# Routing from raw transposes, choices in pieces of 4 and 12 tiles, and two dense steps moved from the prefix to just ahead of the routed experts

## The reference

```
logits = xn @ Wg.T
top_v, top_i = top_k(logits, 2);  gates = softmax(top_v)
pos = running count of earlier choices of the same expert   # kept if pos < cap = 640
h = gelu(inp) * gate                # inp, gate = halves of  x_e @ W1[e]
out[token] += gate * (h @ W2[e])    # for both choices of the token
x + xn + attention(xn) + experts(xn)
```

## Time and profile before

| | |
|---|---|
| median of 3 runs | 143.52 us (142.47 to 145.86) |
| profiled execution, first to last instruction | 141.6 us |
| TensorE busy | 108.6 us, 77% |
| VectorE busy | 93.5 us, 66% |
| ScalarE busy | 68.8 us, 49% |
| GpSimd busy | 75.1 us, 53% |

### The profile page before, as it was taken

How to read it: one execution, slowest core, us unless ns; L and a number is a source line. 1 busy time by engine, 2 the same in 40 slices (tenths; PEclk the granted TensorE clock), 3 DMA queues, 4 the chain that set the end, 5 groups by cost and what they waited for, 6 DMA issues and landing times.

```text
span 141.6 us, 2294 instructions
## 1 busy us (share of the span) xinstructions
PE 108.6 (77%) x705; PEld 97.6 (69%) x705; DVE 93.5 (66%) x299; ACT 68.8 (49%) x164; POOL 75.1 (53%) x92
## 2 busy tenths in 40 slices
PE   0039999999888884898399999999999988965000
PEld 0029769788777763786298999999999987655000
DVE  0699787696576867897337587897757330463991
ACT  0478773346558751323536666767766644410000
POOL 7700707777787787770000277877877777730000
PEclk9999999999999999999959999999999999999755
DMA  3999999999511111114990011111111111696487
GB/s 98 247 329 287 284 370 326 354 347 300 163 42 59 39 64 54 44 59 108 316 283 8 0 56 37 56 58 39 56 58 58 39 56 56 191 306 187 145 237 219
DMA packets 31980, 21.35 MB, mean 151 GB/s; under 512 B 2224, under 2 KB 29872, under 8 KB 31968
## 3 DMA queue, kind: packets, MB, share of 16 engines
q1 hardware_dynamic: 29104, 16.41, 41.3%
q0 software_dynamic: 2144, 4.53, 9.5%
q10 hardware_dynamic: 720, 0.27, 0.8%
HBM read 10.04 MB, written 11.15 MB: 150 GB/s over the span
## 4 chain that ended last, share of the span: by engine, by line
PE 35%; POOL 22%; DVE 13%; issue 11%; DMA 11%; ACT 2%; SPq 1%; POOLq 1%; DVEq 0%; ACTq 0%
POOL y_rows L447 20%; PE bank_h L935 5%; DMA y_last<-rows,target_i 5%; PE bank_h L937 4%; PE bank_h L936 4%; DMA qT<-y_last 3%; PE bank_x L1105 3%; PE bank_y L1047 3%; DMA xs<-in_x 3%; PE bank_x L1016 3%; PE bank_y L956 2%; PE bank_a L956 2%; POOL y_last L447 2%; DVE pre L763 2%; DVE stats L632 2%
## 5 line engine op out<-in xcount | busy, mean ns | idle before, releaser
L447 POOL DMA_INDIRECT y_rows<-rows,target_i x30 | 30.0, 1000 | 25.6 <-ACT rows L588 17.1
L434 POOL DMA_INDIRECT x_slots<-xa,slot_i x32 | 32.6, 1019 | 14.3 <-issue 9.4
L901 DVE TENSOR_TENSOR hid<-gelu,bank_h 128x384 f32<-128x384 f32 (+2 forms) x32 | 16.3, 510 | 19.2 <-ACT gelu L605 19.1
L1157 PE MATMUL bank_y<-w_sb,hid 128*128 128x128 f32 x172 | 21.9, 276 | 2.3 <-issue 2.3
L1157 PEld LDWEIGHTS bank_y<-w_sb,hid 128*128 128x128 f32 x172 | 21.0, 191 | 2.8 <-issue 2.7
L935 PE MATMUL bank_h<-xg_hi,w_lo 128*128 128x384 f32 (+1 forms) x56 | 20.1, 359 | 1.4 <-DVE xg_lo L852 1.2
L605 ACT ACTIVATE gelu<-bank_h 128x384 f32<-128x384 f32 (+2 forms) x32 | 14.7, 459 | 12.0 <-PE bank_h L937 11.2
L937 PE MATMUL bank_h<-xg_hi,w_hi 128*128 128x384 f32 (+1 forms) x56 | 18.0, 321 | 0.0
L936 PE MATMUL bank_h<-xg_lo,w_hi 128*128 128x384 f32 (+1 forms) x56 | 17.9, 320 | 0.0
L588 ACT ACTIVATE rows<-bank_y,gate_slot 128x128 f32<-128x128 f32 x35 | 10.6, 366 | 10.7 <-PE bank_y L1157 10.7
L935 PEld LDWEIGHTS bank_h<-xg_hi,w_lo 128*128 128x128 f32 x56 | 11.1, 197 | 2.0 <-DVE xg_lo L852 1.6
(11 more groups left out here) (156 smaller groups left out, 241.0 us busy)
## 6 DMA issues: line engine op xcount, KB each, us to landing
x_slots<-vacant SPq DMA_DIRECT2D x7, 340.0 KB, 6.7
rows<-x_slots SPq DMA_DIRECT2D x7, 340.0 KB, 5.7
w_raw<-in_w SPq DMA_DIRECT2D x4, 512.0 KB, 7.3
y_rows<-zeros SPq DMA_DIRECT2D x2, 1024.0 KB, 12.2
expo<-y_rows SPq DMA_DIRECT2D x8, 256.0 KB, 7.3
xs<-in_x SPq DMA_DIRECT2D x4, 256.0 KB, 4.5
y_last<-zeros SPq DMA_DIRECT2D x1, 1024.0 KB, 10.9
qT<-y_last SPq DMA_DIRECT2D x4, 256.0 KB, 3.8
```

The source lines that it names most:

```text
L434: nc.gpsimd.indirect_dma_start(x_slots, bass.IndirectOffsetOnAxis(ap=slot_i[:, k, t:t + 1], axis=0), xa[:, t, :], None,).then_inc(rows_out ...
L447: nc.gpsimd.indirect_dma_start(y_rows if r < R - 1 else y_last, bass.IndirectOffsetOnAxis(ap=target_i[:, n:n + 1], axis=0), rows[:, n, 0:D ...
L901: nc.vector.tensor_tensor(hid[s % 2][:, c, 0:cols], gelu[i % 2][:, 0:cols], bank_h[2 * c + 1][:, 0:cols], ALU.mult).then_inc(hid_ready, 1)
L1157: ins = nc.tensor.matmul(bank_y[:, j * D:(j + 1) * D], hid[s % 2][:, c, j * P:(j + 1) * P], w2_sb[:, e, c, :], start=(c == 0), stop=(c == ...
```

## The change

- x itself is transposed as soon as it arrives (`turn_group`). The gate weights are multiplied by a centering matrix (`center`, identity minus 1/128), so that the logits of these transposes are those of xn up to a positive factor per token; the gap between the two best is scaled by `inv1` afterwards. xn is transposed as well, a second time per group, for the QKV products and the dense steps.
- Choices are made in pieces of 4 and 12 tiles. xn of tiles 0 to 7 is made on GpSimd, of 8 to 11 on VectorE, of 12 to 15 on ScalarE.
- `early_product`, `early_results` and `y_early` are gone. The steps are now: two dense, 14 routed, two dense. At the two joints TensorE finishes the step before (`down`) ahead of the next step's `transpose_slots` and `up`.
- SyncE stores the vacant slots ahead of the first weights; the first routed expert's slots are loaded in two transfers. w1's split of expert 0 moves into the QKV loop.

```
-EARLY = 2
-HALVES = 2
+LEAD = 2
+PIECES = ((0, 4), (4, 12))
-    steps = [(e, j0, nj, r) for r, (e, j0, nj) in enumerate(routed_steps)] + all_token_steps[EARLY:]
+    steps = all_token_steps[:LEAD] + [(e, j0, nj, r) for r, (e, j0, nj) in enumerate(routed_steps)] \
+        + all_token_steps[LEAD:]
+    joints = (LEAD, LEAD + len(routed_steps))
...
 TensorE, prefix
             pe.wait_ge(ident_ready, 1)
+            turn_group(0)
+            pe.wait_ge(center_ready, 1)
+            pe.wait_ge(wg_in, 16)
+            nc.tensor.matmul(bank_h[0][:, 0:E], center[:, :], wg_sb[:, :], start=True, stop=True).then_inc(wgc_raw, 1)
+            turn_group(1)
+            pe.wait_ge(wgc_ready, 1)
+            for t in range(GROUP):
+                logits_tile(t)
+            turn_group(2)
+            turn_group(3)
+            for t in range(GROUP, GROUP + 2):
+                logits_tile(t)
+            pe.wait_ge(const_ready, 1)
+            earlier_choices(0)
             transpose_group(0)
+            for t in range(GROUP + 2, T):
+                logits_tile(t)
             transpose_group(1)
+            pe.wait_ge(beta_ready, 1)
+            nc.tensor.matmul(bank_h[3][:, 0:QKV], beta_cols, wqkv_sb[:, :],
+                             start=True, stop=True).then_inc(bias_raw, 1)
             transpose_group(2)
...
             for t in range(T):
-                if t == RESULTS_AT:
+                if t == GROUP - 1:
+                    earlier_choices(1)
+                    transpose_group(3)
                     pe.wait_ge(bias_ready, 1)
-                    early_results(1)
                 qkv_tile(t)
...
 VectorE, prefix
+            statistics(0)
+            statistics(1)
+            statistics(2)
+            inverses(0)
+            statistics(3)
             dve.wait_ge(const_ready, 1)
+            dve.wait_ge(inv1_ready, 1)
             dve.wait_ge(logits_ready, 1)
             choose(0)
+            inverses(1)
+            slots(0)
             gates(0)
+            dve.wait_ge(inv1_ready, 2)
+            nc.vector.scalar_tensor_tensor(nmi[:, 3 * GROUP:T], mv[:, 3 * GROUP:T, 0], -1.0, inv1[:, 3 * GROUP:T],
+                                           ALU.mult, ALU.mult).then_inc(nmi_ready, 1)
+            normalise(2)
+            lower_transposed(0)
+            prepare_wqkv()
             dve.wait_ge(logits_ready, 2)
             choose(1)
+            lower_transposed(1)
+            slots(1)
+            gates(1)
+            dve.wait_ge(std2_ready, 1)
+            link(nc.vector.reciprocal(inv2[:, :], std2[:, :]))
+            nc.vector.tensor_tensor(inv2[:, :], inv2[:, :], std1[:, :], ALU.mult).then_inc(inv2_ready, 1)
+            lower_transposed(2)
             lower_transposed(3)
...
 GpSimd
+            for t in range(2 * GROUP):
+                nc.gpsimd.tensor_scalar(xn[:, t, :], xs[:, t, :], mv[:, t, 0:1], inv1[:, t:t + 1],
+                                        ALU.subtract, ALU.mult).then_inc(xn_pool_ready, 1)
...
 TensorE, steps
             for s in range(S):
-                if s == first_dense:
+                if s in joints:
                     down(s - 1)
+                    if steps[s][3] is not None:
+                        transpose_slots(s)
                 up(s)
-                if s >= 1 and s != first_dense:
+                if s >= 1 and s not in joints:
                     down(s - 1)
```

More of the change, by code:

```diff
@@ L86, in moe_attention_block @@
     for s in range(S):
+        if s in joints and steps[s - 1][3] is None:
+            for j in range(GROUP):
+                note_sum(("step", s - 1), (steps[s - 1][1] + j,))
         for c in range(FC):
[L88 to L95, removed]
+            if (s, c) in FIRST_IN_STEP:
+                g = FIRST_IN_STEP[s, c]
+                note_sum(("first", g), tuple(range(g * GROUP, (g + 1) * GROUP)))
+        if s >= 1 and s not in joints and steps[s - 1][3] is None:
             for j in range(GROUP):
@@ L328, in load_w1 @@
                              w1[2 * i:2 * i + 2].rearrange("e p n -> p e n")).then_inc(w1_in[i], 16)
+            sp.wait_ge(vacant_ready, 2)
+            for r in range(R):
+                sp.dma_start(x_slots_tiles[:, r, :, :], vacant[:, r % 2, :, :]).then_inc(vacant_stored, 16)
             load_w1(0)
@@ L349, in _ @@
             sp.wait_ge(rows_out, 16 * TOP_K * T)
-            for r in range(R):
+            first = PARTS[0][1]
+            sp.dma_start(rows[:, 0:first, :], x_slots_tiles[:, 0, 0:first, :]).then_inc(rows_in[0], 16)
+            sp.dma_start(rows[:, first:ST, :], x_slots_tiles[:, 0, first:ST, :]).then_inc(rows_in_late, 16)
+            for r in range(1, R):
                 sp.dma_start(rows[:, r * ST:(r + 1) * ST, :], x_slots_tiles[:, r, :, :]).then_inc(rows_in[r], 16)
@@ L513, in _ @@
[L513 to L519, removed]
+            nc.scalar.activation(std2[:, :], mv[:, :, 1], ACT.Sqrt, scale=1.0 + LN_EPS,
+                                 bias=eps_sq[:, 0:1]).then_inc(std2_ready, 1)
+            turned(2)
@@ L520, in _ @@
+            nc.scalar.activation(unused[:, :], eps[:, :], ACT.Exp)
+            gap_power(0)
+            turned(3)
+            upper_transposed(0)
+            normalise(3)
             upper_transposed(1)
-            early_gelus(0, 0)
+            act.wait_ge(bias_raw, 1)
+            nc.scalar.activation(bias[:, 0:2 * D], bank_h[3][:, 0:2 * D], ACT.Copy, bias=1.0)
+            nc.scalar.activation(bias[:, 2 * D:QKV], bank_h[3][:, 2 * D:QKV], ACT.Copy).then_inc(bias_ready, 1)
+            gap_power(1)
@@ L968, in earlier_choices @@
+            def earlier_choices(i):
+                pe.wait_ge(assigned_ready, i + 1)
+                before = before_bank[i]
+                t0, nt = PIECES[i]
+                nc.tensor.matmul(before, earlier[:, :], assigned[:, t0:t0 + nt, :], start=True, stop=False)
+                for t in range(t0 + nt - 1):
                     first = max(t + 1, t0)
                     ins = nc.tensor.matmul(before[:, first - t0:, :], ones_bf[:, :],
-                                           assigned[:, t:t + 1, :].broadcast_to((P, t0 + TH - first, E)),
```

413 lines of the change are left out of this document (161 added, 252 removed).

## The result

The changed kernel takes **147.14 us** (median of 4 runs, 146.25 to 148.37), the kernel before, run beside it, 143.00 (4 runs, 141.81 to 145.86). The ratio is 1.028 with a 95% interval from 1.020 to 1.036: slower by 4.1 us, with the lower end of the interval just under two per cent (1.0198). The profiled executions span 145.9 us against 141.6, so +4.3, and the rest of this document accounts for that. In every series the kernel before is run again beside the others, its runs fall into a faster and a slower group, and a ratio is formed from the faster runs alone.

What follows compares the result with a forecast made beforehand. The prediction took GpSimd's result scatters to bound the kernel: first scatter, plus 44.25 us, plus 17.0 of tail. Dense steps +10.6, prefix −3.8 and clock −1.0 gave +5.8, so 143.5 became 149.3 us, range 146.0 to 153.0.

Steps and rivals of the forecast that it cites:

- The dense steps ahead: Between attention and routed steps: two dense steps of 11.2 us, less 0.6 of covered wait, delay the slots' transposes by 10.6.
- The prefix: Before the QKV loop and at its start: the attention ends 3.8 us earlier, bounds 0.6 and 6.6; first product 2.6 earlier.
- The clock ahead of the routed steps: After the attention: dense work without waits may remove the granted clock's dip, gaining 0 to 1.9 us, taken as 1.0.
- Sum to the first scatter: Start of the first result scatter: +10.6 − 3.8 − 1.0 = +5.8 us, with scatters and tail shifting along.
- The earlier slots: Slot scatters before the routed steps: they end near 60 to 62, but 10 us of cover makes this count nothing.
- The predicted gap between the pieces' scatters: On GpSimd, between pieces 0 and 1: a new wait for slots(1), gates(1) and ScalarE's xn at some 29 us.
- What bounds the kernel: At the end: start of first result scatter, plus 44.25 us of scatters, plus 17.0 of tail; TensorE cannot shorten them.
- VectorE and GpSimd side by side: In the prefix, `choose(0)` beside GpSimd's normalisations: one VectorE stall of 0.7 us, from none to three (0 to 2.1) possible.
- A: Rival: the slots set the routed start, transposes come at 65, and the change is faster at 139.3 us; chance 4%.
- B: Rival: VectorE never waits in the prefix and the clock dip is gone, 145.6 us, within 2%; chance 14%.
- C: Rival: the prefix gains nothing, eaten by logits, transposes and stalls; +10, 153.5 us; chance 12%.

Runs made afterwards that it cites:

- e4: The changed kernel with 20 and 8 idle products, results never read, put into TensorE's two waits in the prefix: 145.02 us, ratio 1.013 to the kernel before.
- e1: The changed kernel with all four dense steps behind the routed ones: 146.64 us, ratio 1.029 to the kernel before.
- e8: The changed kernel without its two dense steps ahead of the routed ones (expert 0 for tokens 0 to 1023 not computed): 138.42 us, one run.
- e7: The kernel before without its last two dense steps (expert 0 for tokens 1024 to 2047 not computed): 143.61 us, one run.
- e2: The changed kernel without its two last dense steps (expert 0 for tokens 1024 to 2047 not computed): 143.32 us, one run.
- e6: The changed kernel with all dense steps last, VectorE's adds of fetched rows moved earlier, and 28 idle products in the prefix: 140.92 us, ratio 0.985 to the kernel before.
- e3: The kernel before with only its dense steps moved as in the change, logits, choices and slots as before: 148.11 us, ratio 1.037 to the kernel before.
- e9: The changed kernel, dense order unchanged, with VectorE's adds of fetched rows moved into and ahead of the last dense steps: 145.86 us, one run.

## Why the prediction was right, and where it was not

The forecast was 149.3 us, from 146.0 to 153.0, with 0.82 on slower. The time is 147.14, and it is slower. Taken by its own steps:

- **The dense steps ahead**, +10.6: measured +10.3 (10.89 from the attention's end to the transposes, less the 0.59 that stood there before). The four pieces at the end of the trace were a fair model of the same pieces in the middle, wait for VectorE's adds included. (The prediction put the transposes at 69.16 + 5.8; it should have been 69.16 + 6.8, since the clock's term lies behind them; the sum is not touched.)
- **The prefix**, −3.8: measured −4.64. This is the term that was mis-sized, and inside it two errors nearly cancelled. The first product came 5.5 us earlier, not 2.6, since TensorE's queue for the second piece took 10.5 us and not 12.2 and began 0.9 earlier: VectorE had no stall in `choose(0)`, and transposes, logits, bias and QKV tiles were each a little cheaper. Of that, 0.8 was given back: from the first product to the attention's end the kernel took 35.7 us, before 34.8. e4 says to what, since with the clock kept up it was 32.9. I had costed the clock only for the QKV tiles ahead of the counting, not for the idle stretch behind them.
- **The clock ahead of the routed steps**, −1.0: measured −1.03 from transposes to first scatter (10.12 instead of 11.15). The granted clock behind the transposes' start was 0.66 before (70 to 74) and 1.00 after (74 to 82); in e1 and e8, with no dense step in between, it fell there again (0.57, 0.63 from 66 to 70).
- **Sum to the first scatter**, +5.8: measured +4.63, and the span +4.3.
- **The earlier slots**, nothing: measured nothing. The predicted gap between the pieces' scatters did not appear; slot loads started at 60.67.
- **What bounds the kernel**: here the prediction was only half right. It took the scatters for the one chain that sets the end, and wrote that TensorE "may run ahead of the scatters". TensorE does not run ahead at the end: its last product and VectorE's tail are a second chain, level with the first within 1.2 us before (e7) and 2.3 above it after (e2). The forecast came out because the two lead steps delay both alike, and that was luck: the same reasoning would have promised 135 us for e1, and 144.2 came.
- **VectorE and GpSimd side by side.** The prediction added one stall of 0.7 for VectorE. `choose(0)`'s operations ran at 0.15 to 0.27 beside GpSimd's normalisations, so there was none. The Trainium skill, "SBUF — State Buffer", section "Who interferes with whom", has a VectorE instruction with two SBUF inputs contend with a GpSimd instruction that reads SBUF. In this trace VectorE hardly paid: one operation of `slots(0)` took 0.39 where its neighbours took 0.18 and 0.19. GpSimd took 0.78 us for a normalisation that VectorE does in 0.34; what GpSimd takes for it undisturbed no run here shows.

The trace of the kernel before showed the second chain already, in VectorE's timeline:

```profile
129.55 1.12 DVE L884 SCALAR_TENSOR_TENSOR xs<-bank_y,gate_dense,xs 128x128 f32<-128x128 f32 x4 [2.16 <-PE bank_y L1157]
...
136.87 1.53 DVE L788 TENSOR_TENSOR xs<-xs,qT 128x512 f32<-128x512 f32 x2 [0.18 <-DMA qT<-y_last]
```

VectorE waits for TensorE's last product, adds without a wait, and then stands only 0.18 us for the rows of the last scatters. That short wait is all by which the scatters were the later of the two.

The rivals: A's mechanism is real but far off. The slots would set the start at 63.3 (e6), only once the attention ends before that with nothing ahead. The prediction's argument that the attention cannot end under 62 was a little too strong: it ended at 60.84 in e6. B would have needed TensorE's clock to stay up in the prefix: e4, at 1.013 (1.002 to 1.024), lies within two per cent by its middle. C, a prefix that gains nothing, is refuted by the trace, where the attention ends 4.64 earlier.

Why the change loses is then plain: in the prefix two dense steps cost 5.2 us at the attention's end (e3), so by the difference about half of their 11 us must have lain in time that TensorE would have stood idle. Ahead of the routed experts they cost 9.2 (e8), all of it in both chains. The difference of 4.0 is close to the 4.3 between the spans.

## What to carry to other kernels

When the end is read from one chain, shorten that chain on paper and see which row waits next: here a second chain lay within 1 to 2 us of it, and a rule that fitted both traces failed at the first edit that moved the two apart. Work that fills an engine's idle time is cheap where it stands; before moving it out, price it by what it delays there (5.2 us), not by its own length (11). And look at the clock behind every idle stretch that a change leaves on TensorE: filling two of them with 28 idle products made the kernel 2.1 us shorter by the medians.

## What the runs showed of the hardware that was not expected

Products whose result is never read paid for themselves here: 20 of 512 columns and 8 more kept the granted clock at 1.00 where it was 0.50 to 0.68, and the kernel was 2.1 us shorter by the medians and 2.6 by the spans. The Trainium skill, "TensorE: Matmul & The Clock Gate", section "What's actually happening", says that activity releases the throttle. The trace agrees: 0.91 us of work in the 4 us from 24 to 28 is followed by 0.68 and 0.50, and in e4 4.00 us of work in the same stretch is followed by 1.00.

The clock is also a matter of luck at the margin: at the attention's start (50 to 54) it was 0.58 in the changed kernel, 0.57 in e8 and 1.00 in e1, e2 and e9, with the same program up to there. From VectorE's first product to the attention's end that made 35.7 us against 34.3 to 34.7. In e7, which has the prefix of the kernel before, the clock fell to 0.59 from 58 to 62, where it had been 1.00, and the attention ended at 71.20 instead of 68.57; 2.1 of these 2.6 us stood at the first product already (35.87 instead of 33.74). So single runs are compared here from a common point (transposes or first scatter), not by their spans.

The column of the granted clock does not tell everything ahead of its first fall: in the kernel before it reads 1.00 from 16 to 66, yet a step of 512 columns took 0.43 us at 25.80 and 0.23 at 28.32.
